# Roots and series as scans in the first half's stage code, second half's normalising behind the last join, and ScalarE's tanh ahead of its copies

## The reference

```
x = x + mla(adaln_block(x, cond, ...))          # block below, then causal attention
x = x + ffn(lstm(x, cond, Wx, Wh, b), w1, b1, w2, b2)

_norm(x)     = sqrt(sum(x*x))
logmap0(x)   = arctanh(clip(n, EPS, 1 - 1e-5)) * x / n,  n = _norm(x)
expmap0(v)   = tanh(n) * v / n,                          n = _norm(v)
plin(x,w,b)  = expmap0(logmap0(x) @ w + b)
mobius_add(x, y): num = (1 + 2xy + y2) x + (1 - x2) y;  den = 1 + 2xy + x2 y2

xn = layer_norm(logmap0(x)); xm = expmap0(xn * (1 + sc) + sh)
q, k, v = heads of plin(xm, ...);  softmax attention;  attn_out = plin(...)
x = mobius_add(residual, expmap0(g_msa * logmap0(attn_out)))
... the same with the feed-forward plin(plin(xm, w_f1), w_f2), and mobius_add again
```

## Time and profile before

| | |
|---|---|
| median of three runs | 534.31 us (532.97 to 534.66) |
| profiled execution, device time | 528.99 us |
| its span, first to last instruction | 526.8 us |
| mean granted clock of TensorE | 0.579 |
| busy: TensorE | 398.6 us, 76% |
| busy: VectorE | 367.0 us, 70% |
| busy: ScalarE | 239.8 us, 46% |
| busy: GpSimd | 24.4 us, 5% |
| chain that ended last | TensorE 52%, VectorE 23%, ScalarE 17% |
| first step of the recurrence on VectorE | 142.22 us |

### The profile page before, as it was taken

The page is one execution under the profiler, slowest core; times in us unless marked ns, Lnnn a source line. Parts: engine busy times, 40 slices in busy tenths (PEclk is TensorE's granted clock), DMA queues, the critical chain, the costliest instruction groups (busy, mean ns, idle before and its releaser), DMA issues.

```text
span 526.8 us, 16653 instructions
## 1 busy us (share of the span) xinstructions
PE 398.6 (76%) x6231; PEld 299.0 (57%) x6231; DVE 367.0 (70%) x2234; ACT 239.8 (46%) x940; POOL 24.4 (5%) x42
## 2 busy tenths in 40 slices
PE   2665867595776799995679787887986786977975
PEld 2334645363665576784457565665764575755753
DVE  7887547549588886777867757777777776555553
ACT  1377966564435346335344524434533434423432
POOL 5000700050000000000000000000000000000000
PEclk9776995798555555555555555555555555555555
DMA  7500000000000000000000000000000000000000
GB/s 201 140 0 1 3 3 2 1 1 1 1 2 3 2 1 3 2 2 2 3 2 2 3 3 1 4 3 1 2 5 1 2 3 1 14 7 1 12 11 7
DMA packets 9340, 6.07 MB, mean 12 GB/s; under 512 B 1988, under 2 KB 8620, under 8 KB 9260
## 3 DMA queue, kind: packets, MB, share of 16 engines
q1 hardware_dynamic: 8076, 4.09, 3.1%
q10 hardware_dynamic: 1184, 0.92, 0.5%
HBM read 4.48 MB, written 0.52 MB: 10 GB/s over the span
## 4 chain that ended last, share of the span: by engine, by line
PE 52%; DVE 23%; ACT 17%; issue 6%; DMA 1%; DVEq 0%; ACTq 0%
PE bank L1788 20%; PE bank L1614 8%; DVE bank L1397 6%; ACT hn L838 5%; ACT h_fac L840 5%; DVE vaug L1404 4%; PE bank L1777 3%; PE bank L1687 3%; PE bank L1691 2%; PE bank L1591 2%; PE bank L1565 2%; PE bank L1664 2%; ACT p_mla L788 2%; PE bank L1518 2%; PE bank L1761 1%
## 5 line engine op out<-in xcount | busy, mean ns | idle before, releaser
L1788 PE MATMUL bank<-vaug,wha 128*128 128x4 f16 x2040 | 123.8, 169 | 67.3 <-DVE vaug L1404 65.5
L1788 PEld LDWEIGHTS bank<-vaug,wha 128*128 128x128 f16 x2040 | 94.6, 106 | 133.5 <-DVE vaug L1404 130.5
L838 ACT ACTIVATE hn<-bank 128x16 f32<-128x16 f32 x256 | 51.0, 199 | 148.2 <-PE bank L1788 145.8
L1397 DVE TENSOR_TENSOR_SCAN bank<-hn 128x24 f32<-128x24 f32 x221 | 47.7, 216 | 56.7 <-ACT hn L838 54.0
L1404 DVE TENSOR_TENSOR vaug<-h_fac 128x4 f16<-128x4 f32 x256 | 43.4, 169 | 44.9 <-ACT h_fac L840 42.4
L840 ACT ACTIVATE h_fac<-bank 128x4 f32<-128x4 f32 x221 | 38.9, 176 | 64.2 <-DVE bank L1397 64.2
L1788 PE MATMUL bank<-vaug,whb 128*128 128x4 f16 x1020 | 62.7, 166 | 0.0
L1614 PE MATMUL bank<-kT,qz 32*128 32x32 f32 (+7 forms) x256 | 51.1, 530 | 0.8 <-ACT kT L807 0.4
L1409 DVE TENSOR_TENSOR_SCAN vaug<-h_fac,vaug 128x12 f16<-128x12 f32 x256 | 46.8, 183 | 0.3
L1788 PEld LDWEIGHTS bank<-vaug,whb 128*128 128x128 f16 x1020 | 46.8, 104 | 0.0
L1413 DVE RECIPROCAL hn<-hn 128x4 f32<-128x4 f32 x255 | 41.4, 162 | 0.0
(11 more groups left out here) (301 smaller groups left out, 687.8 us busy)
## 6 DMA issues: line engine op xcount, KB each, us to landing
x_tm<-in_x ACTq DMA_DIRECT2D x1, 512.0 KB, 5.2
x_tb<-in_x SPq DMA_DIRECT2D x4, 128.0 KB, 2.8
wf<-in_L_cond_w_f SPq DMA_DIRECT2D x2, 256.0 KB, 3.3
out_y<-tb SPq DMA_DIRECT2D x7, 64.0 KB, 1.9
ada_w<-in_L_cond_w_ada SPq DMA_DIRECT2D x1, 384.0 KB
ada_b<-in_L_cond_b_ada ACTq DMA_DIRECT2D x1, 384.0 KB, 5.6
wx<-in_L_cond_Wx SPq DMA_DIRECT2D x2, 128.0 KB
wh<-in_L_cond_Wh SPq DMA_DIRECT2D x2, 128.0 KB, 2.5
```

Of the source, the lines that this page charges most:

```text
L838: nc.scalar.activation(gates_out[k], src.rearrange("p (u v b) -> p u v b", u=2, v=2), ACT.Tanh, scale=1.0 / A_SCALE).then_inc(gates_act, 1)
L1397: V.tensor_tensor_scan(cell_of(t).rearrange("p b s -> p (b s)"), cell_in0[:, k].rearrange("p b s -> p (b s)"), cell_in1[:, k].rearrange("p ...
L1788: ins = T.matmul(acc[:, g * B:(g + 1) * B], w[:, g, :], h, start=False, stop=True, skip_group_check=True)
```

## The change

1. The series of the front (for all 8 tiles) becomes one scan of 8 x 7 words: its steps are "state plus 1/k, times the square", and a factor of 0 at the first word of a group starts each tile anew. The table of addends is filled by GpSimd.
2. In the first half (k = 0) `root` becomes two scans, of 10 words a number, over tables that lie in pt_mla; VectorE fills four entries, GpSimd the constants. The marks between its steps go. Readers of the root take it from the table (`root_of`).
3. In the first half the series is one scan of 4 x 7 words.
4. In the first half's joins the results no longer wait one for another; in the last join the first tile is weighed and made before the other three.
5. VectorE: the second half's normed2 and normed3 come behind the first half's "fourth", and `added` behind its end.
6. ScalarE: the first half's tanh of the last join runs before the second half's copies; the second half's squares of "first" and "second" run at the 7th and 19th step of the first causal attention instead of before it and at the 9th.

The second half's own root and series (k = 1) are as before.

```diff
@@ GpSimd @@
+            nc.gpsimd.memset(series_by[:, :, 0], 0.0).then_inc(steps_set, 1)
+            for i in range(SERIES_WORDS):
+                nc.gpsimd.memset(series_add[:, :, i], 1.0 / (15 - 2 * i) if i else 0.0).then_inc(steps_set, 1)
...
+            nc.gpsimd.memset(root_in[:, :, 0:10:9], 0.0).then_inc(steps_set, 1)
+            nc.gpsimd.memset(root_in[:, :, 4:9], 1.0).then_inc(steps_set, 1)
+            nc.gpsimd.memset(root_add[:, :, 1:10], 0.0).then_inc(steps_set, 1)
+            nc.gpsimd.memset(root_end[:, :, 1:10], 0.0).then_inc(steps_set, 1)
+            pool.wait_ge(steps_set, SERIES_WORDS + 5)
+            nc.gpsimd.memset(root_add[:, :, 2], ROOT_K / ROOT_S * 2.38924456).then_inc(steps_set, 1)
+            nc.gpsimd.memset(root_end[:, :, 4], 1.875).then_inc(steps_set, 1)
@@ ScalarE @@
             until(first, "third")
-            until(first, "fourth")
-            until(second, "turned")
             until(first, "end")
-            until(second, "first")
+            until(second, "turned")
...
                 attend(0, i)
-                if i == 8:
+                if i == 6:
+                    until(second, "first")
+                if i == 18:
                     until(second, "second")
@@ VectorE, front @@
-            step(V.tensor_tensor(col(N_SQ), col(ARG), col(ARG), ALU.mult))
+            ratio = col(ARG).unsqueeze(2).to_broadcast([P, TILES, SERIES_WORDS - 1])
+            go(V.tensor_tensor(series_by[:, :, 1:SERIES_WORDS], ratio, ratio, ALU.mult))
             go(V.tensor_scalar(col(IS_SMALL), col(ARG), SERIES_TO, None, ALU.is_lt))
-            step(V.tensor_scalar(col(ALPHA), col(N_SQ), 1.0 / 13, None, ALU.mult))
-            for k in (11, 9, 7, 5, 3):
-                step(V.scalar_tensor_tensor(col(ALPHA), col(ALPHA), 1.0 / k, col(N_SQ), ALU.add, ALU.mult))
+            vec.wait_ge(steps_set, SERIES_WORDS + 1)
+            done()
+            step(V.tensor_tensor_scan(flat(series_out), flat(series_add), flat(series_by), 0.0, ALU.add, ALU.mult))
@@ VectorE, side @@
                 def root(a, y, wide=1):
+                    if k == 0:
+                        n = wide * SIDE
+                        arg = sm[:, k, a:a + wide, :].rearrange("p a n -> p (a n)")
+                        if not roots:
+                            vec.wait_ge(steps_set, SERIES_WORDS + 7)
...
+                        done(late)
+                        on(V.tensor_scalar(root_in[:, 0:n, 1:4].bitcast(I32), arg.bitcast(I32).unsqueeze(2).to_broadcast([P, n, 3]), -0.5, ROOT_BITS,
+                                           ALU.mult, ALU.add))
+                        on(V.tensor_scalar(root_add[:, 0:n, 0], arg, -ROOT_K / ROOT_S, None, ALU.mult))
+                        on(V.scalar_tensor_tensor(root_end[:, 0:n, 0], arg, 0.375, arg, ALU.mult, ALU.mult))
+                        vec.wait_ge(late, counts[id(late)] - 1)
+                        on(V.tensor_tensor_scan(flat(root_mid[:, 0:n]), flat(root_in[:, 0:n]), flat(root_add[:, 0:n]), 0.0, ALU.mult, ALU.add))
+                        on(V.tensor_scalar(root_end[:, 0:n, 2], arg, -1.25, None, ALU.mult))
+                        done(late)
+                        last = ROOT_WORDS * n - 3
+                        on(V.tensor_tensor_scan(flat(root_out[:, 0:n])[:, 0:last], flat(root_mid[:, 0:n])[:, 3:last + 3], flat(root_end[:, 0:n])[:, 0:last],
+                                                0.0, ALU.mult, ALU.add))
+                        yield
+                        return
...
+                    if k == 0 and n:
+                        weighed(0)
+                        done(late)
+                        added(0)
+                        for i in range(1, SIDE):
+                            weighed(i)
+                        done(late)
+                        for i in range(1, SIDE):
+                            added(i)
                         yield
+                    elif k == 0:
+                        for i in range(SIDE):
+                            weighed(i)
+                        done(late)
+                        for i in range(SIDE):
+                            added(i)
+                        yield
@@ VectorE, order of the halves @@
             until(first, "fed")
+            until(first, "fourth")
             until(second, "normed3")
-            until(first, "fourth")
-            until(second, "added")
             until(first, "end")
             go(V.memset(h_fac[:], 0.0))
             until(second, "first")
```

61 lines of the change are left out of this document (43 added, 18 removed).

## The result

The changed kernel takes 530.63 us (median of 7 runs, 528.24 to 531.62), the kernel before, run beside it, 533.26 us (529.67 to 534.66). The ratio is 0.9949, 95% interval 0.9926 to 0.9971: 2.6 us faster. The profiled execution of the changed kernel is its slowest, 531.62 us with a span of 529.2; that of the kernel before was the fastest shown, 528.99 and 526.8. So the two profiles, set side by side, show a kernel that became 2.4 us slower, and have to be read stretch by stretch.

The account below looks back on a forecast made before the run. One dependent chain before the recurrence, which starts at 142.22 us, was taken as the bound. 0.83 + 1.51 + 0.2 = 2.5 us saved, from the median 534.31 to 531.8; range 529.4 to 534.5.

Parts of the forecast that it names:

- three terms: Savings before the recurrence: 0.83 us in the front, 1.51 up to the squares of v_tm, 0.2 in the last stage.
- The front, 0.83: Series at the very front: seven dependent instructions become product, comparison and scan, 1.48 us to 0.65, so 0.83 saved.
- The scans' price: VectorE scans: 0.15 us plus 2.75 ns an element; a root of 4 numbers becomes 0.64 us shorter.
- From the tanh to the squares of v_tm, 1.51: First half, from the first join's tanh: 0.87 us saved by the logarithm's user, plus 0.64 from the next root.
- the 0.64 "turned into a wait": Layer norm's root, 0.64 us: ScalarE's logarithm behind three exponentials limits the saving to 0.87; the rest becomes waiting.
- The last stage, 0.2, between 1.0 and -0.6: Last join to recurrence: 1.0 us saved at TensorE's full clock, 0.6 lost at the far end of half clock, 0.2 taken.
- The choice of the middle: Last stage: 0.2 us saved, taken between its ends since the clock would fall within the pause or the projection.
- in the pause before 121.42: Rival for the last stage: TensorE's clock holds as in this earlier pause; 3.3 us saved, 531.0; chance 0.12.
- The rival with the clock's rise: TensorE's clock rises at 24.8 and before 103.8 by time, not work; about 0.5 us left, 533.8; chance 0.28.
- The slower rival: Feed-forward stretch 103.8 to 118.1 stays at half clock; low until 114 costs 5.3 us, 537.1; chance 0.10.
- GpSimd's fills: Fifteen small fills at about 5.6 to 6.0 and 9.6 to 10.5: counted as nothing, at most 0.7 us lost.

Follow-up runs that it names:

- e4: Changed kernel with the second half's normed2 and normed3 back in front of the first half's last join; 528.57 us, ratio 0.992 to the kernel before.
- e2: Changed kernel without the front's scan and with the old order of the halves; 529.75 us, ratio 0.9953 to the kernel before.
- e14: Changed kernel with e7's unread TensorE products and nothing else; 526.87 us, ratio 0.9886 to the kernel before.
- e13: Kernel before with e7's unread TensorE products and nothing else; 527.84 us, ratio 0.9902 to the kernel before.
- e1: Kernel before with only the front's series as a scan; 532.02 us, ratio 0.999 to the kernel before.
- e5: e4 with GpSimd's fill and selects of gate_cols waiting for VectorE's copy into vbd; 529.18 us, ratio 0.9939 to the kernel before.
- e6: Changed kernel with three unread TensorE products in the pause before the second half's transposes; 527.51 us, ratio 0.9927 to the kernel before.
- e3: Kernel before with only the order of the halves changed on ScalarE and VectorE; 533.57 us, ratio 1.001 to the kernel before.
- e8: Kernel before with GpSimd's selects made to wait for VectorE's copy into vbd; 534.46 us, ratio 1.003 to the kernel before.
- e7: e5 with unread TensorE products in its long pauses and behind the last projection, without e6's place; 523.70 us, ratio 0.9862 to the kernel before.
- e9: e7 with ScalarE's four copies of the second half's v ahead of its tanh again; 521.56 us, ratio 0.9786 to the kernel before.
- e12: e9 with four more unread products ahead of the front's transposes and eight small ones in the tail; 521.25 us, ratio 0.9795 to the kernel before.

## Why the prediction was right

Forecast 531.8 us and faster, by 2.5 us; measured 530.63, 2.6 us under the kernel before in the same rounds. The sum was right; two of its three terms were not exactly so, and they leaned in opposite directions. With the terms as most profiles show them, 0.84 + 2.17 + 0.0, it would be 3.0, which the measured interval (1.5 to 3.9 us) holds as well. That the median came within 0.1 us of the forecast is luck in part: single executions differ by more than the whole saving.

- *The front, 0.83.* The series takes 0.70 us where 0.65 was forecast, the third tile comes 0.84 earlier. Of this 0.68 are there at the first tile (24.16 and 23.48); the rest is the wait of 0.23 for the second tile, which e4's profile has with the new series too and e2's doesn't have with the old. In the pair with unread products (e14 against e13) the tanh of the first join is 0.96 earlier, so the term reaches that far. The timing of e1 alone can't tell it from nothing.
- *The scans' price.* 56 elements took 0.28 us (forecast 0.304), 80 and 77 took 0.33 and 0.32 (0.370 and 0.362), 40 and 37 took 0.24 (0.26 and 0.25). The root of 4 saves 0.69 (0.64 forecast).
- *From the tanh to the squares of v_tm, 1.51.* In the changed kernel's profile 1.59, with VectorE waiting for the logarithm behind three exponentials, as put. But in all eight other executions with the new roots it is 2.14 to 2.19, and that wait is 0.27 (0.31 in e5; in e2, L1278 at 90.40), the bare way over ScalarE. The step that was too small is the 0.64 "turned into a wait": the exponentials start when TensorE's scores are there, at 88.09 in the changed kernel's profile, where the clock was low from before the tanh to 95.5, and at 87.39 in e2, where it came up at 76 and 86. Only in the first were they late enough to hold back the logarithm by more than 0.04 us.
- *The last stage, 0.2, between 1.0 and -0.6.* Measured 0.0 in the profile. Named rightly: the projection in TensorE's queue ahead of the first tile, L1726 directly behind it, half clock after a pause of 3 us. e6 takes the half clock away, and the stage gets 2.34 us shorter than before, more than the upper end of 1.0: 1.25 up to the tile's transpose, and 1.09 behind it, where the clock then also holds and where the sum had no term. The half clock cost the changed kernel 1.33 up to the transpose (10.12 against 8.79), where 1.6 was counted. The choice of the middle was 0.2 too good. What the prediction says for the full clock, that it held "in the pause before 121.42", is misread: TensorE was busy up to that row (L1733, 120.61 plus 0.95), and its last pause before it was 0.35 us, ahead of 119.30. The scans alone (e2) save 1.14 there, the order alone (e3) costs 0.55, and both together 0.0.
- *The rival with the clock's rise* (0.28) can't be seen in the medians: they keep all of the forecast saving. Its sign is in the profiles: the second tile did not stay at 25.0, but the stretch of the first projections ran at half clock, and 2.4 us (23.18 against 20.79) went there. In single executions that is as large as the whole change. e2 shows the same at 22.44, e4 has 20.80, e8 and e13, with the old roots, 23.32 and 22.55: the fall goes with neither form of the roots. Whether the changed kernel has it more often stays open; one profile of each kernel doesn't tell.
- *The slower rival* (0.10) asked for a low clock from 103.8 on through the feed-forward. It was low until 109, in the profile, and that execution is the slowest of the seven, 531.62, yet still under the median before.
- *GpSimd's fills*, costed at nothing, cost nothing that shows; the pair of engines did collide, but at the select that both kernels have.

## What to carry to other kernels

Split a change into its parts before keeping it whole: here the scans alone give as much as the whole change, and the reordering that came with them takes away 1.2 to 1.3 us of the last stage, because TensorE's queue holds a second half's projection ahead of the tile that was hurried. Before work is deferred, ask which queue of another engine has its consumer in front of the very thing that the deferral is to speed up.

When the spread of a kernel's own runs (5.8 us) is larger than the change, compare the distances between the same events in many profiles; 16.8 against 14.6 is plain there, while the spans say the opposite. And look at the granted clock in the pauses first: filling them gave 5 us, twice the change, but only where the added products are over before the next real one is ready.

## What was not expected of the hardware

- The granted clock's falls differ between executions of the same program in the stages before the recurrence, and the column "to sum" follows them to a few tenths. The runs show it too: of the 75 of the kernel before that stood beside the experiments, the 17 with a mean granted clock of 0.578 or 0.579 took 528.85 to 529.79 us, the 29 with 0.572 or 0.573 took 533.51 to 534.68. With the pauses filled the runs of e7, e9 and e14 lie within 1.04, 1.56 and 1.78 us of each other, though those of e12 and e13 within 3.44 and 3.21. Behind the squares of v_tm the way to the sum is 19.26 to 19.27 us in all four kernels where the clock held. All four have the unread products, so what these cost VectorE and ScalarE isn't measured.
- VectorE's copy of 128x512 takes 0.65 or 2.2 us depending on whether it starts 0.05 to 0.1 us before or 0.03 to 0.13 us after a GpSimd select on only 12 partitions, and kernels in which it can't be held up are no faster (e5, e8).
- A scan of 80 elements, 0.33 us, costs less than two dependent instructions on 8 numbers (0.20 apart each). Its price is a line with one exception. The changed kernel's groups, mean ns behind the busy time:

```profile
L1070 DVE TENSOR_TENSOR_SCAN pt_mla<-pt_mla 128x37 f32<-128x37 f32 x4 | 0.9, 238 | 0.1
L1066 DVE TENSOR_TENSOR_SCAN pt_mla<-pt_mla 128x80 f32<-128x80 f32 x2 | 0.6, 324 | 0.0
L940 DVE TENSOR_TENSOR_SCAN pt_mla<-pt_mla 128x56 f32<-128x56 f32 x1 | 0.3, 275 | 0.1
L1262 DVE TENSOR_TENSOR_SCAN pt_mla<-pt_mla 128x28 f32<-128x28 f32 x1 | 0.2, 185 | 0.0
```

From 37 to 80 elements that is 2.0 ns an element, and 56 lie on the same line; the one scan of 28 took some 35 ns less than the line gives, and why stays open. The Trainium skill ("DVE: opcode table, instruction layouts, handler registers and perf-mode slots", section 6) with its half throughput gives the estimate of 2.08 ns that the prediction has; the rows agree with it, and not with the 2.75 that the prediction took from 216 and 183 ns. The trace of before also has 35 scans of 24 elements that write to small and not to bank, at 207 ns; with the same 183 they would have given 2.0.
